# Low parts of the last weights made by products, in a convolution, attention and mixture-of-experts kernel

## The reference, cut to what matters

```python
x = x + W2 @ abs(lowpass(gelu(W1 @ x + b1))) + b2   # 48 hidden channels, a fixed 256 x 256 map per image
t = tokens(x)
n = layernorm(t)
q, k, v = n @ Wq + bq, n @ Wk + bk, n @ Wv + bv     # 12 heads of 16, one key and value head
t = t + attention over the heads of a token (rotary q, k)
n = layernorm(t)
probs = softmax(n @ gate_w.T)                       # 8 experts
p, idx = top_k(probs, 2);  p = p / (sum(p) + 1e-8)
for each token and each of its 2 experts e:
    h = silu(n @ gate_bank[e]) * (n @ up_bank[e])   # 192 -> 384
    t += p_e * (h @ down_bank[e])                   # 384 -> 192
```

## Time and profile before

| what | us |
|---|---|
| median of 3 runs | 404.89 |
| lowest and highest of them | 401.4, 405.83 |
| the profiled execution, its own time | 404.22 |
| its span, first to last instruction | 402.2 |

### The profile page before, as it was taken

How to read it: one execution, slowest core, us unless ns; L and a number is a source line. 1 busy time by engine, 2 the same in 40 slices (tenths; PEclk the granted TensorE clock), 3 DMA queues, 4 the chain that set the end, 5 groups by cost and what they waited for, 6 DMA issues and landing times.

```text
span 402.2 us, 8666 instructions
## 1 busy us (share of the span) xinstructions
PE 358.2 (89%) x2302; PEld 342.7 (85%) x2303; DVE 264.1 (66%) x726; ACT 216.5 (54%) x508; POOL 261.6 (65%) x270
## 2 busy tenths in 40 slices
PE   5987778799986996799999999999999999999990
PEld 4887667688886885699999999999999999999980
DVE  2577758999797997265666666666656666566650
ACT  3475844888561372245555555555555555555540
POOL 3047547788732005457878888887888788888763
PEclk9998898999999865799999999999999999999996
DMA  5999750235554100224544444454444444444432
GB/s 171 260 319 364 264 217 1 93 114 162 157 171 117 9 0 1 69 50 72 75 76 71 81 72 71 70 75 74 74 79 70 70 74 76 70 81 73 72 39 29
DMA packets 39419, 41.07 MB, mean 102 GB/s; under 512 B 13789, under 2 KB 32448, under 8 KB 39392
## 3 DMA queue, kind: packets, MB, share of 16 engines
q0 software_dynamic: 13824, 16.98, 26.0%
q1 hardware_dynamic: 25568, 23.78, 19.2%
HBM read 25.76 MB, written 14.98 MB: 101 GB/s over the span
## 4 chain that ended last, share of the span: by engine, by line
PE 56%; DMA 3%; issue 1%; POOLq 0%; POOL 0%; ACT 0%; DVE 0%; SPq 0%; ACTq 0%; DVEq 0%
PE moe_ps_y L1170 10%; PE moe_ps_h L1156 6%; PE moe_ps_gt L1145 3%; PE moe_ps_gt L1147 3%; PE moe_ps_gt L1149 3%; PE moe_ps_gt L1148 3%; PE moe_ps_gt L1146 3%; PE moe_ps_u L1145 3%; PE moe_ps_u L1148 3%; PE moe_ps_u L1146 3%; PE moe_ps_y L1172 3%; PE moe_ps_u L1149 3%; PE moe_ps_u L1147 3%; PE moe_ps_x L1136 2%; PE moe_ps_x L1137 2%; PE moe_ps_y L1169 2%
## 5 line engine op out<-in xcount | busy, mean ns | idle before, releaser
L1109 POOL DMA_INDIRECT out<-moe_y,idx_map x71 | 112.9, 1591 | 29.0 <-issue 20.1
L1101 POOL DMA_INDIRECT moe_xt<-rows,idx_map x71 | 74.3, 1046 | 54.8 <-POOLq L926 28.3
L1254 ACT ACTIVATE moe_yy<-moe_ps_y,moe_xt 128x384 f32<-128x384 f32 x71 | 41.4, 583 | 70.3 <-PE moe_ps_y L1170 70.3
L1170 PE MATMUL moe_ps_y<-wd,moe_h_hi 128*128 x213 | 70.0, 353 | 0.6 <-DVE moe_h_lo L1326 0.5
L1334 DVE TENSOR_TENSOR moe_y<-moe_yy 128x192 f32<-128x192 f32 x71 | 25.5, 360 | 55.8 <-ACT moe_yy L1254 55.8
L1234 ACT ACTIVATE moe_x_hi<-moe_ps_x 128x256 fp32r<-128x256 f32 x71 | 27.3, 385 | 38.8 <-PE moe_ps_x L1137 38.8
L1310 DVE TENSOR_TENSOR moe_x_lo<-moe_ps_x,moe_x_hi 128x128 fp32r<-128x128 f32 x71 | 20.7, 292 | 32.1 <-ACT moe_x_hi L1234 32.1
L1326 DVE TENSOR_TENSOR moe_h_lo<-moe_ps_h,moe_h_hi 128x384 fp32r<-128x384 f32 x71 | 39.6, 558 | 2.7 <-ACT moe_h_hi L1246 0.6
L1170 PEld LDWEIGHTS moe_ps_y<-wd,moe_h_hi 128*128 128x128 f32 x213 | 40.2, 189 | 1.2 <-issue 1.2
L1320 DVE TENSOR_TENSOR moe_hid<-moe_ps_u,moe_sg 128x384 f32<-128x384 f32 x71 | 38.9, 548 | 0.0
L1172 PE MATMUL moe_ps_y<-wd,moe_h_lo 128*128 x142 | 35.5, 250 | 0.0
(11 more groups left out here) (230 smaller groups left out, 968.1 us busy)
## 6 DMA issues: line engine op xcount, KB each, us to landing
w_lo<-in_wgu SPq DMA_DIRECT2D x8, 768.0 KB, 15.7
xs<-in_x SPq DMA_DIRECT2D x8, 388.0 KB, 8.6
rows<-front_xr SPq DMA_DIRECT2D x8, 384.0 KB, 2.7
out<-xs SPq DMA_DIRECT2D x8, 384.0 KB, 3.5
wd<-in_down SPq DMA_DIRECT2D x8, 288.0 KB, 4.3
xta<-in_xT SPq DMA_DIRECT2D x8, 256.0 KB, 5.5
moe_xt<-rows,idx_map POOLq DMA_INDIRECT x71, 2.8
out<-moe_y,idx_map POOLq DMA_INDIRECT x71, 3.6
```

What stands on the lines that cost most here:

```text
L1101: nc.gpsimd.indirect_dma_start(xt[:, slot, :], None, rows.ap(), bass.IndirectOffsetOnAxis(ap=idx_map[:, j, 0:1], axis=0)).then_inc(gathere ...
L1109: nc.gpsimd.indirect_dma_start(out, bass.IndirectOffsetOnAxis(ap=idx_map[:, j, 1:2], axis=0), y[:, j % YR, :], None, compute_op=ALU.add).t ...
L1170: ins = nc.tensor.matmul(both, hi, halves, start=(k == 0), stop=(k == 2))
L1254: nc.scalar.activation(yy[:, s].rearrange("p h c -> p (h c)"), ps_y[:, s, 0:2 * C], ACT.Copy, scale=xt[:, slot, bass.ds(GC + e, 1)]).then_ ...
```

## The change

1. For the last two quads (`APART = 2`) EPS and the negated mean are made on VectorE (`late_parts`, behind the aggregation) instead of GpSimd.
2. The low parts of experts 5 to 7 (three of `w_lo[:, e, 0]`, three of `w_lo[:, e, 1]`, three of `wd`) are no longer made by VectorE, neither the three at the end of the front nor the six at the head of the experts. In the routing phase TensorE adds, in PSUM, the identity times the value in fp32 and the negated identity times the high part, in pieces of 512 columns and the rest, and ScalarE copies the sum to its place. For the `w_lo` parts the second product is fp32r, for `wd` both are fp32. There are two PSUM slots. Three parts come ahead of the counts in place of the 10 fillers, six behind them, with 8 fillers in place of 30.
3. ScalarE makes the negated identity first, converts the ones early, and waits for the triangle alone, which has a semaphore of its own.
4. From the second round of the one-hot loop on, two products of 64 columns whose result is not used come ahead of the wait.
5. At the head of the experts there are 24 fillers instead of 11, and TensorE and ScalarE wait for `change_done` (a small VectorE instruction) instead of `ready`.

```diff
+APART = 2
+AHEAD_OF_COUNTS = 3
...
                 def deviation(q):
...
+                    if q < QUADS - APART:
+                        pool.wait_ge(mv_done, made(q))
+                        pool.sem_inc(pool_turn, 1)
+                        nc.gpsimd.tensor_scalar(vtmp[:, s, :], mv[:, s, :, 1], EPS, None, ALU.add).then_inc(eps_done, 1)
+                        nc.gpsimd.tensor_scalar(minus[:, s, :], mv[:, s, :, 0], -1.0, None, ALU.mult).then_inc(mean_done, 1)
+                        pool.wait_ge(eps_done, made(q))
+                    else:
+                        pool.wait_ge(parts_done, q - (QUADS - APART) + 1)
...
+                def late_parts(q):
+
+                    s = q % RING
+                    dve.wait_ge(mv_done, made(q))
+                    dve.wait_ge(dev_done, freed(q))
+                    nc.vector.tensor_scalar(vtmp[:, s, :], mv[:, s, :, 1], EPS, None, ALU.add)
+                    nc.vector.tensor_scalar(minus[:, s, :], mv[:, s, :, 0], -1.0, None, ALU.mult).then_inc(parts_done, 1)
...
                     scores(n)
                     if n:
                         residual(n - 1)
+                    if n > QUADS - APART:
+                        late_parts(n - 1)
                     weights(n)
...
                 residual(last)
+                late_parts(last)
...
-                for e in range(READY, EXPERTS):
-                    split(e)
...
+        parts = []
+        for e in range(READY, EXPERTS):
+            parts += [(w_lo[:, e, 0], wa_hi[:, e]), (w_lo[:, e, 1], wb_hi[:, e]), (wd[:, e, 1], wd[:, e, 0])]
...
+                sp.dma_start(trit[:], tri).then_inc(tri_in, 16)
                 for dst, src in consts:
                     sp.dma_start(dst[:], src).then_inc(consts_in, 16)
...
+                def low_part(n):
+
+                    low = parts[n][0]
+                    act.wait_ge(low_made, n + 1)
+                    nc.scalar.activation(low, ps_low[:, n % RING, 0:low.shape[1]], ACT.Copy).then_inc(low_out, 1)
+
+                nc.scalar.activation(neg[:], eye[:], ACT.Copy, scale=-1.0).then_inc(negated, 1)
+                act.wait_ge(filled, 1)
+                nc.scalar.activation(oner[:], ones[:], ACT.Copy)
                 act.wait_ge(diff_done, 1)
                 nc.scalar.activation(pr[:, EARLY:T], lg[:, EARLY:T], ACT.Exp)
+                low_part(0)
                 act.wait_ge(second_done, 1)
                 nc.scalar.activation(red[:, 5, EARLY:T], red[:, 4, EARLY:T], ACT.Exp).then_inc(ex_done, 1)
+                act.wait_ge(tri_in, 16)
+                nc.scalar.activation(trir[:], trit[:], ACT.Copy).then_inc(exact, 1)
+                for n in range(1, len(parts)):
+                    low_part(n)
                 act.wait_ge(consts_in, 16 * len(consts))
-                act.wait_ge(filled, 1)
-                nc.scalar.activation(oner[:], ones[:], ACT.Copy)
-                nc.scalar.activation(trir[:], trit[:], ACT.Copy).then_inc(exact, 1)
...
-                keep_busy(10)
+                def low_product(n):
+
+                    low, high = parts[n]
+                    width = low.shape[1]
+                    if n >= RING:
+                        pe.wait_ge(low_out, n + 1 - RING)
+                    for at in (slice(0, 512), slice(512, width)):
+                        into = ps_low[:, n % RING, at]
+                        nc.tensor.matmul(into, eye[:], low[:, at].bitcast(F32), start=True, stop=False)
+                        minus = (neg[:], high[:, at]) if n % 3 < 2 else (neg[:].bitcast(F32), high[:, at].bitcast(F32))
+                        ins = nc.tensor.matmul(into, *minus, start=False, stop=True)
+                    ins.then_inc(low_made, 1)
+
+                pe.wait_ge(negated, 1)
+                for n in range(AHEAD_OF_COUNTS):
+                    low_product(n)
                 pe.wait_ge(exact, 1)
                 pe.wait_ge(chosen, 1)
...
-                keep_busy(30)
+                for n in range(AHEAD_OF_COUNTS, len(parts)):
+                    low_product(n)
+                keep_busy(8)
...
                 for q in range(TILES // HT):
                     s = q % HR
+                    if q:
+                        for _ in range(2):
+                            nc.tensor.matmul(ps_p[:, 0:64], order_of, order_of[:, 0:64], start=True, stop=True)
                     pe.wait_ge(hot_a_done, q + 1)
...
-                keep_busy(11)
+                keep_busy(24)
                 turn_x(0, 0)
                 keep_busy(4)
-                pe.wait_ge(ready, 1)
+                pe.wait_ge(change_done, 1)
...
                 nc.scalar.activation(sg[:, 0, 0:1], eye[:, 0:1], ACT.Silu)
-                act.wait_ge(ready, 1)
+                act.wait_ge(change_done, 1)
...
-                for e in range(READY, EXPERTS):
-                    for low, high in ((w_lo[:, e, 0], wa_hi[:, e]), (wd[:, e, 1], wd[:, e, 0])):
-                        ins = nc.vector.tensor_tensor(low, low.bitcast(F32), high.bitcast(F32), ALU.subtract)
-                ins.then_inc(ready, 1)
```

More of the change, by code:

```diff
@@ L140, in program @@
                         x, xT, w1, w2, lowpass, wgu, down, ytab, ident, wqkv, gate, rope, iotas[1], out)
-            routing_phase(nc, lg, choice, tri, iotas, row_tiles, idx_map, e_j, out, scattered)
+            routing_phase(nc, lg, choice, tri, iotas, row_tiles, idx_map, e_j, out, scattered, eye, wa_hi, wb_hi, w_lo, wd)
         expert_phase(nc, eye, rows, out, wa_hi, wb_hi, w_lo, wd, idx_map, e_j, scattered)
@@ L224, in front_phase @@
         early_chain = a.sem("early_chain")
+        parts_done = a.sem("parts_done")
         early_less, early_second, early_ex, early_chosen, early_gates = (
@@ L682, in deviation @@
                     pool.wait_ge(pow_done, made(q))
-                    pool.wait_ge(mean_done, made(q))
+                    if q < QUADS - APART:
+                        pool.wait_ge(mean_done, made(q))
                     pool.sem_inc(pool_turn, 1)
@@ L887, in choose_experts, with routing_phase @@
     tt2(gates[:, at], tmp[:], tmp2[:], ALU.add).then_inc(gates_done, 1)
-def routing_phase(nc, lg, choice, tri, iotas, row_tiles, idx_map, e_j, out, scattered):
+def routing_phase(nc, lg, choice, tri, iotas, row_tiles, idx_map, e_j, out, scattered, eye, wa_hi, wb_hi, w_lo, wd):
     E, T = EXPERTS, TILES
@@ L917, in routing_phase @@
         ps_p, ps_t, ps_m = (a.ps(n, [P, 512]) for n in ("ps_p", "ps_t", "ps_m"))
+        neg, ps_low = a.sb("neg", [P, P], F32R), a.ps("ps_low", [P, RING, 1024])
+        negated, low_made, low_out, tri_in = (a.sem(n) for n in ("negated", "low_made", "low_out", "tri_in"))
+        parts = []
+        for e in range(READY, EXPERTS):
+            parts += [(w_lo[:, e, 0], wa_hi[:, e]), (w_lo[:, e, 1], wb_hi[:, e]), (wd[:, e, 1], wd[:, e, 0])]
         consts_in, gates_out, filled = (a.sem(n) for n in ("consts_in", "gates_out", "filled"))
@@ L923, in routing_phase @@
         hot_done, hot_a_done, map_done = a.sem("hot_done"), a.sem("hot_a_done"), a.sem("map_done")
-        consts = [(trit, tri)] + list(zip((io, first, idp, no_row, no_place), iotas[:1] + iotas[2:]))
+        consts = list(zip((io, first, idp, no_row, no_place), iotas[:1] + iotas[2:]))
         with nc.Block() as block:
@@ L1087, in expert_phase @@
         x_hi_done, x_lo_done, x_lob_done = a.sem("x_hi_done"), a.sem("x_lo_done"), a.sem("x_lob_done")
-        ready, change_done = a.sem("ready"), a.sem("change_done")
+        change_done = a.sem("change_done")
         silu_done, hid_done, weighed = a.sem("silu_done"), a.sem("hid_done"), a.sem("weighed")
```

## The result

| | before | after |
|---|---|---|
| median of 4 runs each, us | 403.36 | 413.1 |
| lowest and highest | 401.4, 405.83 | 410.95, 414.71 |
| profiled execution, its span | 404.22, 402.2 | 413.35, 411.3 |

The ratio is 1.0263, with a 95% interval of 1.0217 to 1.031: the change made the kernel slower by 2.6%.

The account below looks back on a forecast made before the run. The prediction took a serial stretch from the front's end through counts, one-hot loop, map and first gather to the first tile as the bound; +0.2 + 0.7 - 1.3 = -0.4 took the median from 404.89 to 404.5 us, range 400.8 to 409.7.

Parts of the forecast that it names:

- Two extra products per round: One-hot loop: extras fill TensorE's idle time and hold the clock, last round 0.36 earlier, net map delay +4.1 us.
- a rival at 8%: One-hot loop: extras don't hold the clock, a round costs TensorE 1.85 us over VectorE's 0.971; 414 to 418, chance 8%.
- 24 fillers: Expert head: fillers at 0.17 us each run to 163.5 and set the first transpose, +0.7 us.
- my rival on the head: Between loop and head fillers: the clock falls while TensorE has nothing; 406.1 if it returns, 409.8 if not; chance 22%.
- the low products: Routing phase on TensorE: 1.64 us for a gate and up part, 2.15 for a down part, priced by columns.
- the one-hot loop's start: Routing phase: low products and eight fillers move the first one-hot product to 143.0 from 137.78.
- VectorE's fifth round: One-hot loop: it waits for TensorE's first round, 143.8 instead of 139.34; the loop ends 4.45 us later.
- the first tile at full clock: First expert tile: at 2.4 GHz the gate product takes 1.12 instead of 1.96 and transposes 0.45 less, -1.3 us.
- The front's +0.2: Front: statistics of the last two quads moved from GpSimd to VectorE cost +0.2 us, bounds -0.5 to +0.5.
- the gather is held by VectorE's subtractions: Expert head: without the six subtractions the first gather takes 0.98 us instead of 5.63, -4.65.
- the cheap products: Routing phase rival: wide fp32 products run at the fp32r price, map some 2.5 us earlier; about 397.7, chance 10%.
- the worst head: Expert head: the clock doesn't come back, 24 fillers take 8.1 us and the 1.3 is lost; +5.3, 409.8.

Follow-up runs that it names:

- wide_extras: The changed kernel with the two extra products per round 128 columns wide instead of 64; 403.35 us, ratio 0.9952 to the kernel before.
- no_extras: The changed kernel without the two extra products per round of the one-hot loop; 403.99 us, ratio 1.0068 to the kernel before.
- narrow_extras_alone: The kernel before with only the two extra 64-column products per round added; 410.38 us, ratio 1.0134 to the kernel before.
- wide_eleven: The changed kernel with 128-column extra products and 11 fillers at the head instead of 24; 400.6 us, ratio 0.9935 to the kernel before.
- six_products: The changed kernel with 128-column extras, 11 head fillers, six low products instead of nine, three splits back on VectorE; 397.0 us, ratio 0.9869 to the kernel before.
- no_head_subtractions: The kernel before without the six VectorE subtractions at the head of the experts, their low parts left as loaded; 398.27 us, ratio 0.9896.
- subtractions_back: The changed kernel with six subtractions of the same shapes put back on VectorE at the head, results unused; 416.14 us in one run.
- six_products_warm_tail: six_products with eight more 128-column products behind the last one-hot product; 395.75 us, ratio 0.9862 to the kernel before.

## Why the prediction was wrong, step by step

**The step that failed** is "Two extra products per round ... What they should give is the clock". My sum held the loop to be VectorE's because the extras "are issued before the wait, so they fill TensorE's idle time", and took a full TensorE to be a warm one. The records do show it full, 1.00 in every window, and the clock falls nevertheless. I had the outcome as a rival at 8%, with 1.85 for a round at half clock (1.70 measured) and 414 to 418 (413.1 measured). Against it I put that TensorE "is idle a few per cent"; this reason was wrong in kind, for wide_extras fills the windows no more and keeps the clock. The routing phase lost 12.5 where I had 4.1, and no_extras gives 8.6 of it back. Why products of 64 columns don't hold the clock where 128 do isn't settled by these runs; that the width makes the difference is shown by wide_extras, which changes nothing else, and that the clock falls beside narrow ones without any other part of the change by narrow_extras_alone. Wide ones alone, in the kernel before, were not tried.

**The second failure is a term with the clock in it**: 24 fillers "at 0.17 each" to 163.5. They began at 0.50 and took 7.09: the condition of my rival on the head came true, at nearly its worst case (8.1). From the read of the map to the first transpose I had 163.5 - 157.25 = 6.25, and it was 9.09. The rows were there at 165.96 + 2.90 = 168.9, an estimate from the wide_eleven rows, and the fillers held the transpose 4.1 longer. That is where the gather's gain went. At half clock eleven instead of 24 bring the transpose 6.98 - 3.45 = 3.5 nearer to the gather; how much of that reaches the whole time the ratios don't tell.

**Right, by size:** the low products (1.74 and 1.63 where I had 1.64; 127.80 - 125.72 = 2.08 for 2.15); the one-hot loop's start, +4.70 for 5.2; VectorE's fifth round with its wait of 3.61 for "some 4"; the first tile at full clock, -1.25 for -1.3 (by luck: I had the clock warm throughout, and it came back only at the end of the slow fillers, near 172); the counts, which came at 6.09 after the front's end for 5.70 before, +0.39 for +0.49. The front's +0.2 can't be told from nothing. The ends of my range don't follow from the sums: no case but the cheap products goes below the forecast's 402, where the range begins at 400.8, and the worst head gives 409.8 for 409.7.

**Right, by mechanism:** the gather is held by VectorE's subtractions: 5.63 in every profiled kernel with the six subtractions, 1.05 or 1.06 in every one without. The Trainium skill infers the opposite in "SBUF — State Buffer", section "Who interferes with whom" (a subtraction of two SBUF tensors would leave the write side of the port free). The same section of the Trainium skill also states, and the prediction overlooked it, that a VectorE instruction with two SBUF inputs contends with a GpSimd instruction that reads SBUF; the gather reads its `idx_map` there. The measurement agrees with this sentence: the gather is held. Whether it is held at the read of its indices or at the writing of its descriptors, which the inference was about, no run here shows.

**What I overlooked** is that the three splits at the end of the front were free, as the prediction itself says, and that making them by products cost 3 x 1.63 us of TensorE time on the path to the one-hot loop. six_products leaves them where they were, and the 4.7 is gone. So the idea of the change is good for 1.3% (no_head_subtractions, which only leaves the six subtractions out, gains 1.0%); the narrow extras above all, the three needless parts and, by the traces, the long row of fillers turned it into a loss of 2.6%.

## What to carry to other kernels

Price any work that is added to keep TensorE warm at 1.2 GHz too: if it fits into the loop only at 2.4, it turns a clock that didn't matter into the bound, and here the loop without it was nearly as fast at half clock as a warm one (the map 29.6 and 29.2 us after the start of the phase). Count the fillers ahead of a transfer against the transfer that they cover, at the lower clock, again whenever the transfer gets shorter. And before work is moved, see which part of it was hidden already and leave that part where it is.

## What the runs showed of the hardware that I had not expected

A TensorE whose records fill every window can still be granted 1.2 GHz: with two fp32 products of 64 columns beside four of 72 per round the clock fell in every profiled execution (changed kernel, subtractions_back, narrow_extras_alone), with two of 128 columns it stayed at 2.4 GHz through the loop in all four (wide_extras, wide_eleven, six_products, six_products_warm_tail); a round took 0.89 at 2.4 GHz with either. The same pause of 2.33 us after a warm loop ended once at 0.50 (wide_extras) and once at 1.00 (wide_eleven); one of 2.24 ended at 0.50 (six_products). An indirect gather on GpSimd takes 1.05, and 5.63 when six subtractions of 0.74 to 0.94 begin on VectorE at nearly the same moment, ending 0.93 after the last of them.
